# One weight change per subject: where x3T, the two roundings of W0 and their waits stand in the queues

## The chip, the cores and the metric

The kernel runs on one core of one Trainium2 chip. The metric is device time in microseconds (us) of one execution, as the median of several. Times inside an execution are counted from the start of the profiled span.

## The reference, cut to what matters

`x` is 128 samples of 128 tokens with 512 features, float32. Each sample has a subject (8 of them), a category (64), a language and a `delta_t`. Four conditioned layers follow each other, each with a residual:

```python
x = x + (x @ W0[subject].T + b0[subject])
x = x + rotate_pairs(x, a * cos(ang), a * sin(ang))   # pairs of tokens, angle and gain from delta_t
x = x + (x @ W2[category] + b2[category])
h = relu(x @ W1[language] + b1[language])
x = x + layernorm(x + h @ Wup[language] + bup[language]) * gamma[language] + beta[language]
```

## The kernel before, in words

Samples are worked one after another, sorted by subject, so that the weights of the first layer, W0 (512 x 512), are fetched, prepared and kept for all samples of a subject. A table in SBUF, made by the kernel itself, says for each place in the order whether the subject changes there (`is_first`) and how many subjects have begun (`ordinal_of`); engines read it into registers. With 8 subjects there are 7 changes after the start.

Float32 products of layers 0 and 2 are made from two parts in a faster format: ScalarE rounds a tile to its `hi` part, another engine subtracts to get the `lo` part, and TensorE adds x_hi·w_hi, x_lo·w_hi and x_hi·w_lo. Both weight matrices have the identity added first (GpSimd, `fold_w0`, `fold_w2`), which gives the residual. Weights are rounded and subtracted in two halves of 1024 columns.

The five instruction queues are written out by hand, and each works its own in order; they meet at semaphores. Step `s` of the main loop does this:

- **TensorE** (from L825): `l0_front(s + 1)`, the 4 products x_hi·w0_hi (L740) and half of x_lo·w0_hi (L744); `l2(s)`, 12 products (L779, L783, L789, the last 4 waiting for w2_lo by halves); `l0_back(s + 1)`, the other half of x_lo·w0_hi (L751) and x_hi·w0_lo (L757); the transpositions of x3 (L799); `up(s - 1)` (L818); `rotate(s + 1)` (L768), which needs x1 of sample s + 1; `down(s)` (L809), which needs x3T. Then the next step.
- **ScalarE** (from L519): relu (L500), x_hi of sample s + 2 (L458), the diagonal for rotate (L451), w2_hi of s + 1 in two halves (L486), then at a change of subject `round_w0(s + 2)`: under a branch, waits for the folded W0, for layer 0 of s + 1 to be done and for x1 of s + 1; two halves of w0_hi (L462) and a copy of the bias b0 (L463). Then x3T (L507) and x2T_hi of s + 1 (L493).
- **VectorE** (from L687): x2T_lo (L644), w2_lo in two halves (L629), mix (L604), `centre(s - 2)` (L668), x3 of s, called `finish_l2` (L651), yb (L679), x1 of s + 1 (L637), `statistics(s - 1)` (L657, L659, L661: y, bn_stats, bn_aggr), and at a change `rest_of_w0(s + 2)` (L610, w0_lo in two halves).
- **GpSimd** (from L418): rstd (L387, L391), then, once w2_lo of step s is made, x_lo of s + 2 (L381) and the fold of W2 of s + 2 (L375); x3 + bup (L398), + beta (L405), at a change the fold of W0 of s + 3 (L369).
- **SP** issues all loads and stores, up to four samples ahead; the next W0 is fetched into the same buffer once w0_lo and the copy of b0 of the present one are made (`load_w0`, L243).

That x1 of the sample before must be made ahead of the new b0 is because `finish_l0` adds `b0_sb` (L637). That TensorE doesn't use the new w0_hi too early was given by x3T, which ScalarE copied after it, and w0_lo by w2_lo, which VectorE made after it.

## Time and profile before

| | |
|---|---|
| median of 3 runs | 1203.55 us (1201.64 to 1204.3) |
| the profiled execution's own time | 1206.43 us |
| its span | 1204.6 us |
| TensorE matmul busy | 1133.4 us, 94% |
| VectorE busy | 1025.5 us, 85% |
| GpSimd busy | 865.6 us, 72% |
| ScalarE busy | 583.4 us, 48% |
| mean granted TensorE clock | 0.98 |

The span is the time from the first to the last instruction of the execution that the profiler took; the execution's own time is 1.8 us longer. PE is TensorE's matmuls, PEld its weight loads, DVE VectorE, ACT ScalarE, POOL GpSimd, SPq the queue of SyncE. The clock is a share of 2.4 GHz; an average below 1 over a stretch means that it was at 1.2 GHz in part of it. In the profile a buffer's number is left out of its name, so `w_hi` is w0_hi at L462 and w2_hi at L486, and `x` at L651 is x3, at L637 x1.

### The profile page before, as it was taken

The numbers are of one execution on the slowest core, as the hardware profiler recorded it, in microseconds if no ns is written. First come the engines' busy times: TensorE is split into PE (matmuls) and PEld (weight loads), VectorE is DVE, ScalarE is ACT, GpSimd is POOL, SyncE is SP. The second block draws the span as 40 slices with busy tenths as digits, with TensorE's granted clock in tenths as the row PEclk, the third lists the DMA queues.
The fourth block names the chain that finished last, engine by engine and source line by source line (L and its number), as shares of the span: only waits on it lengthen the run. The fifth ranks groups of instructions, "written<-read, shape, count | busy, mean of one in ns | idle before, by whom it ended". The sixth has DMA issues, their size and how long they took to land.

```text
span 1204.6 us, 27886 instructions
## 1 busy us (share of the span) xinstructions
PE 1133.4 (94%) x5902; PEld 913.2 (76%) x5902; DVE 1025.5 (85%) x1465; ACT 583.4 (48%) x923; POOL 865.6 (72%) x792
## 2 busy tenths in 40 slices
PE   1899999999989999999998999989999999999996
PEld 1678878878768887877886788778787887777874
DVE  3398888998888898898888888988888888898887
ACT  2345455455455555445454545445445544544542
POOL 3966667886676677668767666876766677768884
PEclk9899999999999999999999899999998999999999
DMA  6967776777787687767767786787678678867772
GB/s 241 426 225 233 254 258 211 238 253 221 224 291 238 208 261 263 252 213 239 251 215 274 231 259 208 232 286 239 211 249 280 208 237 247 275 214 247 243 252 79
DMA packets 96407, 291.70 MB, mean 242 GB/s; under 512 B 11584, under 2 KB 11712, under 8 KB 78272
## 3 DMA queue, kind: packets, MB, share of 16 engines
q1 hardware_dynamic: 96192, 289.52, 73.3%
q14 instruction: 164, 1.34, 0.3%
q8 instruction: 51, 0.84, 0.3%
HBM read 255.93 MB, written 33.55 MB: 240 GB/s over the span
## 4 chain that ended last, share of the span: by engine, by line
SPq 37%; PE 34%; issue 18%; DVE 5%; DMA 2%; POOL 2%; DVEq 1%; ACT 1%; POOLq 0%; ACTq 0%
SPq L193 6%; SPq L199 5%; SPq L205 5%; PE ps_l L789 4%; PE ps_l L757 4%; PE ps_l L740 4%; PE ps_l L779 4%; PE ps_y L818 3%; PE ps_l L783 3%; PE ps_hT L809 3%; PE ps_mix L768 3%; SPq L196 3%; SPq L208 3%; SPq L202 3%; SPq L286 3%
## 5 line engine op out<-in xcount | busy, mean ns | idle before, releaser
L629 DVE TENSOR_TENSOR w_lo<-w_in,w_hi 128x1024 fp32r<-128x1024 f32 x256 | 330.2, 1330 | 0.0
L381 POOL TENSOR_TENSOR x_lo<-x_in,x_hi 128x512 fp32r<-128x512 f32 x128 | 166.0, 1297 | 160.4 <-DVE w_lo L629 157.1
L486 ACT ACTIVATE w_hi<-w_in 128x1024 fp32r<-128x1024 f32 x256 | 255.3, 1045 | 12.4 <-PE ps_l L783 12.4
L375 POOL TENSOR_TENSOR w_in<-w_in,ident 128x512 f32<-128x512 f32 x128 | 164.3, 1284 | 65.2 <-DMA w_in<-W 64.8
L451 ACT ACTIVATE ps_diag<-ident,cos 128x128 f32<-128x128 f32 x128 | 47.6, 372 | 304.9 <-DVE mix L604 304.6
L405 POOL TENSOR_TENSOR x<-x,beta_sb 128x512 f32<-128x512 f32 x128 | 174.3, 1361 | 28.9 <-POOL x3b L398 28.9
L768 PEld LDWEIGHTS ps_mix<-mix,x 128*128 128x128 f32 x1024 | 132.7, 191 | 73.4 <-issue 69.5
L398 POOL TENSOR_TENSOR x3b<-x,bup_sb 128x512 f32<-128x512 f32 x128 | 169.0, 1320 | 9.6 <-DVE x L651 9.6
L740 PE MATMUL ps_l<-w_hi,x_hi 128*128 128x512 f32 x512 | 154.8, 425 | 15.4 <-ACT w_hi L462 14.1
L789 PE MATMUL ps_l<-w_lo,x2T_hi 128*128 128x512 f32 x512 | 147.7, 401 | 11.6 <-DVE w_lo L629 11.4
L809 PE MATMUL ps_hT<-x3T,w_in 128*128 128x128 f32 x1024 | 138.7, 279 | 13.8 <-ACT x3T L507 13.8
L657 DVE TENSOR_TENSOR ps_y<-ps_y,x3b 128x512 f32<-128x512 f32 x128 | 89.5, 699 | 70.4 <-PE ps_y L818 68.8
L493 ACT ACTIVATE x2T_hi<-ps_mix 128x512 fp32r<-128x512 f32 x128 | 76.3, 596 | 145.5 <-PE ps_mix L768 145.5
L768 PE MATMUL ps_mix<-mix,x 128*128 128x128 f32 x1024 | 136.1, 276 | 7.8 <-DVE x L637 7.6
L779 PE MATMUL ps_l<-w_hi,x2T_hi 128*128 128x512 f32 x512 | 141.0, 398 | 0.0
L809 PEld LDWEIGHTS ps_hT<-x3T,w_in 128*128 128x128 f32 x1024 | 127.0, 195 | 15.7 <-issue 15.7
L757 PE MATMUL ps_l<-w_lo,x_hi 128*128 128x512 f32 x512 | 138.4, 392 | 0.0
L783 PE MATMUL ps_l<-w_hi,x2T_lo 128*128 128x512 f32 x512 | 138.1, 392 | 0.2 <-DVE x2T_lo L644 0.2
L818 PE MATMUL ps_y<-wup_sb,hT 128*128 x256 | 131.1, 594 | 0.8 <-ACT hT L500 0.8
L789 PEld LDWEIGHTS ps_l<-w_lo,x2T_hi 128*128 128x128 f32 x512 | 92.7, 189 | 45.8 <-DVE w_lo L629 29.3
L391 POOL TENSOR_TENSOR rstd<-var_eps,minus_half 128x1 f32<-128x1 f32 x128 | 107.5, 840 | 18.9
L651 DVE TENSOR_TENSOR x<-ps_l,b_in 128x512 f32<-128x512 f32 x128 | 88.5, 692 | 34.3 <-PE ps_l L789 33.8
(82 smaller groups left out, 1713.6 us busy)
## 6 DMA issues: line engine op xcount, KB each, us to landing
w_in<-W SPq DMA_DIRECT2D x128, 1024.0 KB, 6.3
b_in<-b SPq DMA_DIRECT2D x136, 256.0 KB, 5.8
x_in<-xT SPq DMA_DIRECT2D x128, 256.0 KB, 4.8
w_in<-W SPq DMA_DIRECT2D x128, 256.0 KB, 2.7
out<-yb SPq DMA_DIRECT2D x128, 256.0 KB, 5.4
w_in<-W0T SPq DMA_DIRECT2D x8, 1024.0 KB, 4.9
bup_sb<-bup SPq DMA_DIRECT2D x1, 2560.0 KB, 8.8
wup_sb<-Wup SPq DMA_DIRECT2D x1, 2560.0 KB, 10.6
```

The lines of the kernel that those rows point to most:

```text
L398: pool.tensor_tensor(x3b[s % 2][:, :], x3[s % X3B][:, :], bup_sb[:, bass.ds(lang * D, D)], ALU.add)\
L405: pool.tensor_tensor(x3[s % X3B][:, :], x3[s % X3B][:, :], beta_sb[:, bass.ds(lang * D, D)], ALU.add)\
L486: act.activation(w2_hi[:, halves[n]], w2_in[s % WB][:, halves[n]], ACT.Copy).then_inc(w2_hi_made, 1)
L629: dve.tensor_tensor(w2_lo[:, half], w2_in[s % WB][:, half], w2_hi[:, half].bitcast(fp32), ALU.subtract).then_inc(w2_lo_made, 1)
L740: pe.matmul(ps_l0[:, :], x_hi[s % 2][:, c * N:(c + 1) * N], w0_hi[:, c * D:(c + 1) * D], start=(c == 0), stop=False)
L757: mm = pe.matmul(ps_l0[:, :], x_hi[s % 2][:, c * N:(c + 1) * N], w0_lo[:, c * D:(c + 1) * D], start=False, stop=(c == C - 1))
L768: mm = pe.matmul(ps_mix[:, c * N:(c + 1) * N], x1[:, c * P:(c + 1) * P], mix[:, :], start=True, stop=True)
L779: pe.matmul(ps_l2[:, :], x2T_hi[:, c * N:(c + 1) * N], w2_hi[:, c * D:(c + 1) * D], start=(c == 0), stop=False)
L783: mm = pe.matmul(ps_l2[:, :], x2T_lo[:, c * N:(c + 1) * N], w2_hi[:, c * D:(c + 1) * D], start=False, stop=False)
L789: mm = pe.matmul(ps_l2[:, :], x2T_hi[:, c * N:(c + 1) * N], w2_lo[:, c * D:(c + 1) * D], start=False, stop=(c == C - 1))
L809: mm = pe.matmul(ps_hT[:, :], w1_in[s % 2][:, c * A:(c + 1) * A], x3T[:, c * N:(c + 1) * N], start=(c == 0), stop=(c == C - 1))
L818: pe.matmul(ps_y[s % 2][:, :], hT[:, :], wup_sb[:, bass.ds(lang * D, D)], start=True, stop=True)\
```

## The change

ScalarE copies x3T ahead of `round_w0`, and there waits for x1 only before the copy of b0. VectorE makes w0_lo of sample s + 1's subject in step s, between `centre` and `finish_l2`, instead of at the end of step s − 1. TensorE gets waits of its own on w0_hi, b0 and w0_lo, by halves and against the ordinal of the subject, which it reads into a register once per step, between rotate and down; the waits of samples 0 and 1 (both halves of w0_hi; the diagonal) go. w0_lo has a semaphore for each half.

```diff
@@ -155,7 +155,7 @@
         coef_made = sem("coef_made")
         w0_folded = sem("w0_folded")
         w0_hi_made = [sem(f"w0_hi_made{half}") for half in range(2)]
-        w0_lo_made = sem("w0_lo_made")
+        w0_lo_made = [sem(f"w0_lo_made{half}") for half in range(2)]
         b0_made = sem("b0_made")
         x_hi_made = sem("x_hi_made")
         x_lo_made = sem("x_lo_made")
@@ -228,7 +228,8 @@
             sp.dma_start(b1_sb[:, :], b1T).then_inc(b1_loaded, 16)
             sp.dma_start(bup_sb[:, :], bup.rearrange("l d -> (l d)").partition_broadcast(P)).then_inc(bup_loaded, 16)
 
-            sp.sem_inc(w0_lo_made, 2)
+            sp.sem_inc(w0_lo_made[0], 1)
+            sp.sem_inc(w0_lo_made[1], 1)
             sp.sem_inc(b0_made, 1)
             sp.wait_ge(ids_made, 2)
 
@@ -245,7 +246,7 @@
 
                 first, sub, ordinal = is_first(sp, s), subject_of(sp, s), ordinal_of(sp, s)
                 with sp.If(first):
-                    sp.wait_ge(w0_lo_made, 2 * ordinal)
+                    sp.wait_ge(w0_lo_made[1], ordinal)
                     sp.wait_ge(b0_made, ordinal)
                     fetch_w0(sub)
 
@@ -457,24 +458,24 @@
                 act.wait_ge(x_loaded[s % XB], landed(s, XB))
                 act.activation(x_hi[s % 2][:, :], x_in[s % XB][:, :], ACT.Copy).then_inc(x_hi_made, 1)
 
-            def convert_w0():
+            def convert_w0(s):
                 for n, half in enumerate(halves):
                     act.activation(w0_hi[:, half], w0_in[:, half], ACT.Copy).then_inc(w0_hi_made[n], 1)
+                if s >= 1:
+                    act.wait_ge(x1_made, s)
                 act.activation(b0_sb[:, :], b0_in[:, :], ACT.Copy).then_inc(b0_made, 1)
 
-            def round_w0(s):
+            def round_w0(s, first):
 
                 if s == 0:
                     act.wait_ge(w0_folded, 1)
-                    convert_w0()
+                    convert_w0(s)
                     return
-                first = is_first(act, s)
                 with act.If(first):
                     ordinal = ordinal_of(act, s)
                     act.wait_ge(w0_folded, ordinal)
                     act.wait_ge(l0_done, s)
-                    act.wait_ge(x1_made, s)
-                    convert_w0()
+                    convert_w0(s)
 
             def round_w2(s, n):
 
@@ -507,13 +508,13 @@
                 act.activation(x3T[:, :], ps_x3T[:, :], ACT.Copy).then_inc(x3T_made, 1)
 
             round_x(0)
-            round_w0(0)
+            round_w0(0, None)
             make_diag(0)
             round_w2(0, 0)
             round_w2(0, 1)
             round_x(1)
             round_x2T(0)
-            round_w0(1)
+            round_w0(1, is_first(act, 1))
             make_diag(1)
             act.wait_ge(b1_loaded, 16)
 
@@ -528,9 +529,10 @@
                 if s < LAST:
                     round_w2(s + 1, 0)
                     round_w2(s + 1, 1)
+                first = is_first(act, s + 2) if s < LAST - 1 else None
+                copy_x3T(s)
                 if s < LAST - 1:
-                    round_w0(s + 2)
-                copy_x3T(s)
+                    round_w0(s + 2, first)
                 if s < LAST:
                     round_x2T(s + 1)
             relu_hT(LAST, language_of(act, LAST))
@@ -608,7 +610,7 @@
                 for n, half in enumerate(halves):
                     dve.wait_ge(w0_hi_made[n], ordinal)
                     dve.tensor_tensor(w0_lo[:, half], w0_in[:, half], w0_hi[:, half].bitcast(fp32),
-                                      ALU.subtract).then_inc(w0_lo_made, 1)
+                                      ALU.subtract).then_inc(w0_lo_made[n], 1)
 
             def rest_of_w0(s, first):
 
@@ -690,11 +692,13 @@
                 rest_of_w2(s, 1)
                 if s < LAST:
                     make_mix(s + 1)
-                first = is_first(dve, s + 2) if s < LAST - 1 else None
+                first = is_first(dve, s + 1) if 1 <= s < LAST else None
                 if s == 2:
                     dve.wait_ge(gamma_loaded, 16)
                 if s >= 2:
                     centre(s - 2)
+                if 1 <= s < LAST:
+                    rest_of_w0(s + 1, first)
                 finish_l2(s)
                 if s >= 2:
                     finish_norm(s - 2)
@@ -707,8 +711,6 @@
                     dve.wait_ge(coef_made, 4)
                 if s >= 1:
                     statistics(s - 1)
-                if s < LAST - 1:
-                    rest_of_w0(s + 2, first)
             centre(LAST - 1)
             finish_norm(LAST - 1)
             statistics(LAST)
@@ -726,17 +728,14 @@
             pe.matmul(ps_mix[:, 0:B], dt_wide, onehot, start=True, stop=True).then_inc(sorted_done, 1)
             pe.wait_ge(ids_made, 2)
 
-            def l0_front(s):
-
-                if s == 0:
-                    pe.wait_ge(w0_hi_made[0], 1)
-                    pe.wait_ge(w0_hi_made[1], 1)
-                if s == 1:
-                    pe.wait_ge(diag_made, 2)
+            def l0_front(s, ordinal):
+
                 if s >= 1:
                     pe.wait_ge(x1_made, s)
                 pe.wait_ge(x_hi_made, s + 1)
                 for c in range(C):
+                    if c in (0, C // 2):
+                        pe.wait_ge(w0_hi_made[c // (C // 2)], ordinal)
                     pe.matmul(ps_l0[:, :], x_hi[s % 2][:, c * N:(c + 1) * N], w0_hi[:, c * D:(c + 1) * D],
                               start=(c == 0), stop=False)
                 pe.wait_ge(x_lo_made, s + 1)
@@ -744,16 +743,15 @@
                     pe.matmul(ps_l0[:, :], x_lo[s % 2][:, c * N:(c + 1) * N], w0_hi[:, c * D:(c + 1) * D],
                               start=False, stop=False)
 
-            def l0_back(s):
-
+            def l0_back(s, ordinal):
 
                 for c in range(C // 2, C):
                     pe.matmul(ps_l0[:, :], x_lo[s % 2][:, c * N:(c + 1) * N], w0_hi[:, c * D:(c + 1) * D],
                               start=False, stop=False)
-                if s == 0:
-                    pe.wait_ge(b0_made, 2)
-                    pe.wait_ge(w0_lo_made, 4)
+                pe.wait_ge(b0_made, ordinal + 1)
                 for c in range(C):
+                    if c in (0, C // 2):
+                        pe.wait_ge(w0_lo_made[c // (C // 2)], ordinal + 1)
                     mm = pe.matmul(ps_l0[:, :], x_hi[s % 2][:, c * N:(c + 1) * N], w0_lo[:, c * D:(c + 1) * D],
                                    start=False, stop=(c == C - 1))
                 mm.then_inc(l0_done, 1)
@@ -820,17 +818,18 @@
 
             pe.wait_ge(dt_made, 1)
             pe.wait_ge(consts_made, 3)
-            l0_front(0)
-            l0_back(0)
+            l0_front(0, 1)
+            l0_back(0, 1)
             rotate(0)
+            ordinal = ordinal_of(pe, 1)
 
             for s in range(B):
                 lang_before = language_of(pe, s - 1) if s >= 1 else None
                 if s < LAST:
-                    l0_front(s + 1)
+                    l0_front(s + 1, ordinal)
                 l2(s)
                 if s < LAST:
-                    l0_back(s + 1)
+                    l0_back(s + 1, ordinal)
                 transpose_x3(s)
                 if s == 1:
                     pe.wait_ge(wup_loaded, 16)
@@ -838,6 +837,8 @@
                     up(s - 1, lang_before)
                 if s < LAST:
                     rotate(s + 1)
+                if s < LAST - 1:
+                    ordinal = ordinal_of(pe, s + 2)
                 down(s)
             up(LAST, language_of(pe, LAST))
 
```

## Rows read from the trace of the kernel before

**Rows 1.** The page, busy time, share of the span and instructions.

```profile
PE 1133.4 (94%) x5902; PEld 913.2 (76%) x5902; DVE 1025.5 (85%) x1465; ACT 583.4 (48%) x923; POOL 865.6 (72%) x792
```

**Rows 2.** Timeline of an ordinary step (start, length, engine; idle before).

```profile
175.61 1.08 PEld L768 LDWEIGHTS ps_mix<-mix,x 128*128 128x128 f32 x8 [0.45 <-issue]
...
176.98 0.60 ACT L493 ACTIVATE x2T_hi<-ps_mix 128x512 fp32r<-128x512 f32 x1 [1.16 <-PE ps_mix L768]
...
181.99 0.69 DVE L651 TENSOR_TENSOR x<-ps_l,b_in 128x512 f32<-128x512 f32 x1 [0.24 <-PE ps_l L789]
```

**Rows 3.** x3 in ordinary steps, then around the first, fourth, last change: first, last start.

```profile
L651 DVE TENSOR_TENSOR x<-ps_l,b_in x3: 692/692/692, 173.4 to 190.5; 128x512 f32<-128x512 f32 x3
...
L651 DVE TENSOR_TENSOR x<-ps_l,b_in x2: 691/692/692, 161.6 to 173.4; 128x512 f32<-128x512 f32 x2
...
L651 DVE TENSOR_TENSOR x<-ps_l,b_in x2: 692/692/692, 657.5 to 673.2; 128x512 f32<-128x512 f32 x2
...
L651 DVE TENSOR_TENSOR x<-ps_l,b_in x2: 692/692/692, 1048.3 to 1060.3; 128x512 f32<-128x512 f32 x2
```

**Rows 4.** Waits of the whole run: us in total, times, longest.

```profile
DVE x L651 <- PE ps_l L789: 33.8, 79, 7.3
...
PE ps_hT L809 <- ACT x3T L507: 13.8, 7, 2.0
...
ACT w_hi L462 <- DVE x L637: 11.6, 7, 2.8
...
DVE w_lo L610 <- issue: 5.4, 7, 1.3
```

**Rows 5.** Timeline of the third change, and one row of the fourth.

```profile
479.16 2.00 ACT L462 ACTIVATE w_hi<-w_in 128x1024 fp32r<-128x1024 f32 x2 [1.70 <-DVE x L637]
...
481.22 3.69 DVE L610 TENSOR_TENSOR w_lo<-w_in,w_hi 128x1024 fp32r<-128x1024 f32 x2 [0.61 <-issue]
...
481.84 1.99 POOL L405 TENSOR_TENSOR x<-x,beta_sb 128x512 f32<-128x512 f32 x1 [0.23 <-POOL x3b L398]
...
482.07 0.58 ACT L493 ACTIVATE x2T_hi<-ps_mix 128x512 fp32r<-128x512 f32 x1
...
484.83 0.68 DVE L644 TENSOR_TENSOR x2T_lo<-ps_mix,x2T_hi 128x512 fp32r<-128x512 f32 x1
...
485.43 2.34 DVE L629 TENSOR_TENSOR w_lo<-w_in,w_hi 128x1024 fp32r<-128x1024 f32 x2
...
487.70 0.33 DVE L604 SCALAR_TENSOR_TENSOR mix<-signed_swap,sin,ps_diag 128x128 f32<-128x128 f32 x1
...
487.86 1.30 POOL L381 TENSOR_TENSOR x_lo<-x_in,x_hi 128x512 fp32r<-128x512 f32 x1 [2.20 <-DVE w_lo L629]
...
489.11 1.29 POOL L375 TENSOR_TENSOR w_in<-w_in,ident 128x512 f32<-128x512 f32 x1
...
489.27 0.69 DVE L651 TENSOR_TENSOR x<-ps_l,b_in 128x512 f32<-128x512 f32 x1 [0.57 <-PE ps_l L789]
...
661.95 1.13 PE L768 MATMUL ps_mix<-mix,x 128*128 128x128 f32 x8 [1.91 <-DVE x L637]
```

**Rows 6.** SP's issue of a W2 tile at the third change, and its landing (KB, us).

```profile
481.42 0.33 SPq L264 DMA_DIRECT2D w_in<-W  x1
...
w_in<-W SPq DMA_DIRECT2D x1, 1024.0 KB, 6.5
```

**Rows 7.** First and sixth change: us, PE, PEld, DVE, ACT, POOL busy, PEclk, DMA share, GB/s.

```profile
160.00:173.00 13.00, 10.41 (x50) 7.30 (x50) 10.95 (x16) 6.86 (x11) 7.23 (x8) 1.00 0.70 231
921.00:936.00 15.00, 12.20 (x49) 9.65 (x48) 11.15 (x14) 7.39 (x12) 11.54 (x11) 0.77 0.81 276
```

**Rows 8.** Register loads of TensorE (each step) and ScalarE (the ordinal): ns min/median/max.

```profile
L202 PEldq TENSOR_LOAD <-ids x128: 296/302/957, 44.8 to 1194.1; - x128
...
L208 ACTq TENSOR_LOAD <-ids x7: 273/291/1142, 161.7 to 1049.2; - x7
```

**Rows 9.** Timeline near the start, GpSimd.

```profile
33.20 15.63 POOL L416 TENSOR_TENSOR x<-stats_cols,x 128x96 f32<-128x96 f32 x1
```


## The prediction

> **What bounds the kernel now.** I read the page first: TensorE is busy 94% of the span [rows 1]. The timeline of an ordinary step shows that this isn't the whole bound [rows 2]. The step repeats every 8.55 us (x3 at 173.4, 182.0 and 190.5, [rows 2, 3]). TensorE's weights for rotate are loaded as soon as x1 is there, at 175.61, and it has no hole from there to the next x3. VectorE waits for TensorE for only 0.24 us before the next x3. Two chains of nearly equal length close in every step, so delay put on either one counts.
>
> The seven changes of subject cost extra. There the distance from one x3 to the next is 11.8 us in the first (161.6 to 173.4), 15.7 in the fourth and 12.0 in the seventh and last [rows 3]; the seven together are 94.6 us, 34.8 over seven steps of 8.54. Outside this sum, 2.9% of the time, there is little for the change to win.
>
> The waits name what happens [rows 4]: ScalarE waits 11.6 us for x1 before it rounds W0, `down` then waits 13.8 us for x3T behind it, both seven times. The timeline of the third change gives the order [rows 5]: w0_hi 479.16, x2T_hi 482.07 (0.58 long), w0_lo 481.22 to 484.91, x2T_lo 484.83, w2_lo 485.43, mix 487.70, x3 489.27. So w0_lo holds VectorE back while x2T_hi is already there, and the wait of `down` is not itself the end of the chain.
>
> **The change, part by part.** *ScalarE.* The same four operations (x3T, two halves of w0_hi, b0) still stand ahead of x2T_hi; they take 2.91 us from the first start to x2T_hi [rows 5]. What goes is the wait for x1. What comes is the taken branch and its load of the ordinal, formerly hidden behind that wait: VectorE shows 0.6 to 1.3 us for the same pair (5.4 over seven, [rows 4]), of which x3T's 0.5 us covers most; I take 0.3, between 0 and 0.8. Release to start costs another 0.1. So 11.6 − 7 × 0.4 = 8.8 us. It loses 0.7 where the transposition ends up to 0.3 us after w2_hi, and 0.7 where rotate, which starts with x1, ends too late: in the fourth change rotate runs 661.95 to 663.08 [rows 5], so x2T_hi can start at 663.2 and not at 662.5, where ScalarE's own work would have it. **x2T_hi comes earlier by 7.4 us in total.** b0 keeps the wait for x1, which has ended by then.
>
> *VectorE.* w0_lo leaves the place ahead of x2T_lo and stands, one step of TensorE's order later, between centre and the next x3. Old, from x2T_hi's start to that x3: 7.20 us in the third change (482.07 to 489.27) and 51.5 over all seven. New: 0.69 to x2T_lo (x2T_hi's 0.60 and a release), 2.87 to mix (484.83 to 487.70), then w0_lo in series. Here GpSimd matters, since it starts x_lo 0.16 us after mix, for 1.30, and then folds the next W2 for 1.29 [rows 5]. That the two engines don't run such operations side by side is seen where w0_lo meets the beta addition: 3.69 us for the pair of halves and 1.99 for the addition, while a pair alone takes 2.34 (w2_lo). So the first half starts when x_lo ends (mix + 1.46) and ends at mix + 2.6; the second ends at + 3.8 if the fold has not landed by then, and at + 5.0 if it has and takes its turn. In the third change x2T_hi comes 1.2 us earlier, at 480.9, mix at 484.4, and mix + 2.6 is 487.0; the tile to be folded is issued at 481.42 and lands 6.5 us later, at 487.9: no collision [rows 6]. Worked out likewise three of the seven collide, and two more miss by under 0.3 us. Seven times 0.69 + 2.87 + 3.85, plus 3 × 1.25, is 55.6. **This chain gets 4.1 us longer**; with no collision at all it would be 3.1 shorter (3.35 in place of 3.85), with all seven 9.1 longer.
>
> *Clock.* Over the sixth change the granted clock is 0.77 on average, which is partly 1.2 GHz and partly 2.4, over the first 1.00 [rows 7]. The first has one long idle time of TensorE, before `down`; the others have two close together, as 1.91 us before rotate in the fourth [rows 5] and 2.0 before `down` [rows 4]. The loss is small in the old order (x3 waits for TensorE 0.57 us in the third change, 0.24 in an ordinary step), because VectorE is late there in any case. The new order takes away the idle before `down`, but TensorE now stops ahead of the w0_lo products: done with its x_lo part at mix + 0.95, it gets the first half at + 2.6, the second at + 3.8 or + 5.0, and x3 for its transpositions after that. That is 2.7 to 4 us idle in 3.6 to 4.9. I expect about five falls, now just before work that has no slack: the gapless step. A stretch like the old ones, of 3 to 4 us at 1.2 GHz, halves what is done in it and costs 1.3 to 1.7. **+7.0 us**, between 0 and 15. The Trainium skill ("TensorE: Matmul & The Clock Gate", Part 1: The HAM clock gate) gives the half rate as the state after a whole idle stretch of its monitor. By that rule pieces of idleness broken by matmuls would leave the clock up, and the sum would be about 1200.8 us; rows 7 with rows 5 speak against it, since the clock fell with rotate between two idle times.
>
> *Every step.* The untaken branch leaves the place between bn_aggr and x2T_lo, some 0.1 us where VectorE binds (it does in 49 of 128 steps, since TensorE releases x3 in 79, [rows 4]); most of those exceed 8.54 by less: −1.0, between 0 and −5. TensorE gets one more register load per step, between rotate and down, and register waits. A load takes 0.30 us, at most 0.96 [rows 8], and with its arithmetic and check about 0.65; rotate's passes occupy 1.0 us after 0.25 us of issue. It just fits, and the load for the language behind it as well; only the odd long ones show. +1.5 us, between 0 and 12 (0.1 in each of 120 steps). ScalarE's load and branch lie before its idle 1.16 us for rotate [rows 2]: nothing. SP's wait uses a count reached many samples before: nothing.
>
> *Start.* `l0_front(0)` no longer waits for both halves, and `l0_front(1)` not for diag; that is at most some 4 us by x3 of sample 0. Both are swallowed: x_lo of sample 2, without which `l0_front(2)` can't go on, stands behind GpSimd's power of 15.63 us, which ends at 48.8 whatever TensorE does [rows 9]. 0, between −1.5 and +1.5.
>
> **Sum:** −7.4 + 4.1 + 7.0 − 1.0 + 1.5 = +4.2 us on the profiled execution's 1206.43 (span 1204.6), 2.9 above the median shown; on the median 1203.55 that is 1207.8. A measurement of this kernel can tell about 0.2%, 2.4 us, from no change.
>
> **The rivals.**
> *The clock stays up* (0.20). Everything as above without the 7 us: 1200.8, range 1198 to 1203. For it: the 2 us before `down` in the first change left the clock at full [rows 7]. Against it: the new idle pieces are longer and closer.
> *The ports don't collide and the clock stays* (0.10). w0_lo takes 2.35 us directly behind centre: 48.4 for the chain, 3.1 less than before, and 7.4 + 3.1 + 1.0 − 1.5 = 10.0 us gained: 1193.6. Against it is the 3.69 beside 2.34 [rows 5].
> *The effects cancel* (0.20). Falls of the clock, fewer or half covered by the idle time, cost 2 to 5 us: 1202 to 1206. The change then only moves the same stall from `down` to the w0_lo products.
> *TensorE's queue* (0.10), the far side. The load between rotate and down, with the wait behind it, delays the first weights of down. rotate is issued only as x1 arrives, so the queue starts each step empty. It decides from a delay of 0.05 us per step, and 0.1 gives +12: 1219 with the rest. In this place the gapless step [rows 2] has no cover.
> *Code behind the taken branch*, part of the forecast's upper range: ScalarE's load of the ordinal took up to 1.14 us, with a median of 0.29 [rows 8]. If each taken branch of ScalarE showed 1.3 us, x2T_hi would lose 7 us: 1214.8. The Trainium skill ("Runtime: NRT & Kernel Launch", Instruction fetch mechanics) says that a taken branch out of the fetched pages stalls until its page is loaded; no row here shows that as a rule: VectorE's seven waits add up to only 5.4 us.
>
> **How the numbers follow.** Forecast as worked out: 0.40, its own range 1204 to 1215. Faster is the two first rivals, 0.30; same is the cancelling one and the forecast's low edge, 0.22; slower the rest, 0.48. The range leaves out the far ends of the second and fourth rival: 1196 to 1216.
>
> **What would show it.** `down` no longer waits for x3T; x2T_hi stands 0.1 to 1.7 us nearer to the x3 before it; w0_lo follows centre and its pair takes 2.8 us or more; TensorE's longest waits at a change are for w0_lo of W0; the granted clock is below 1 after the new x3 and no more before it; ordinary steps stay at 8.54. The forecast is wrong if x3 to x3 falls under 12.5 us in all seven changes, if the clock stays at 1.00 there, or if ordinary steps grow.

## The result, and the profile after

The changed kernel takes 1215.13 us (median of 9 runs, 1206.18 to 1217.9), the kernel before beside it 1202.43 (9 runs). The ratio is 1.0091, with a 95% interval of 1.0071 to 1.0111: **slower by 10.9 us**, where 4.2 were forecast. The profiled execution took 1216.06 us, 9.6 more than that of before.

The head of its page:

```profile
span 1214.2 us, 28514 instructions
...
PE 1137.1 (94%) x5902; PEld 916.4 (75%) x5902; DVE 1011.1 (83%) x1465; ACT 585.8 (48%) x923; POOL 842.1 (69%) x792
```

The busy times are those of before [rows 1] within 0.5% on TensorE and ScalarE; VectorE's is 1.4% lower and GpSimd's 2.7%. Less busy time makes no kernel slower, so look at waits and at order. TensorE's waits:

```profile
PE ps_l L755 <- DVE w_lo L612: 20.5, 15, 2.0
PE ps_l L739 <- ACT w_hi L463: 13.2, 1, 13.2
...
PE ps_mix L766 <- DVE x L639: 8.8, 7, 1.9
```

The 13.8 us of `down` behind x3T [rows 4] are gone, and 20.5 us in 15 pieces have come, in which the w0_lo products wait for VectorE (the 13.2 is the start). The timeline of the third change, the answer to [rows 5] (start us, us, engine and line):

```profile
479.25 0.69 DVE L653 TENSOR_TENSOR x<-ps_l,b_in 128x512 f32<-128x512 f32 x1 [0.43 <-PE ps_l L787]
...
481.73 2.00 ACT L463 ACTIVATE w_hi<-w_in 128x1024 fp32r<-128x1024 f32 x2
...
484.38 0.60 ACT L494 ACTIVATE x2T_hi<-ps_mix 128x512 fp32r<-128x512 f32 x1
...
485.45 1.29 POOL L406 TENSOR_TENSOR x<-x,beta_sb 128x512 f32<-128x512 f32 x1 [0.23 <-POOL x3b L399]
...
485.68 3.28 DVE L631 TENSOR_TENSOR w_lo<-w_in,w_hi 128x1024 fp32r<-128x1024 f32 x2
...
488.89 0.33 DVE L606 SCALAR_TENSOR_TENSOR mix<-signed_swap,sin,ps_diag 128x128 f32<-128x128 f32 x1
...
489.81 4.11 DVE L612 TENSOR_TENSOR w_lo<-w_in,w_hi 128x1024 fp32r<-128x1024 f32 x2
490.58 2.25 POOL L376 TENSOR_TENSOR w_in<-w_in,ident 128x512 f32<-128x512 f32 x1
...
491.85 0.70 PE L755 MATMUL ps_l<-w_lo,x_hi 128*128 128x512 f32 x2 [1.64 <-DVE w_lo L612]
...
493.85 0.68 DVE L653 TENSOR_TENSOR x<-ps_l,b_in 128x512 f32<-128x512 f32 x1
...
493.98 1.06 PE L755 MATMUL ps_l<-w_lo,x_hi 128*128 128x512 f32 x2 [1.42 <-DVE w_lo L612]
...
495.68 1.92 PE L816 MATMUL ps_y<-wup_sb,hT 128*128 x2
```

The order is the one the change wants. But VectorE and GpSimd now meet twice: w2_lo meets the beta addition (3.28 us for a pair of halves that takes 2.34 alone, [rows 5]), and w0_lo meets x_lo and the fold (4.11). And behind the new x3 the up-projection takes 1.92 us where it took 1.02 one step earlier: TensorE runs at 1.2 GHz. That is so around every new x3 of a change. The windows (length, busy times of TensorE, its weight loads, VectorE, ScalarE and GpSimd, then the granted clock):

```profile
173.00:181.00 8.00, 6.03 (x25) 4.23 (x26) 6.05 (x8) 1.63 (x3) 4.29 (x5) 0.79 0.59 208
354.00:362.00 8.00, 5.87 (x24) 4.07 (x25) 6.21 (x8) 1.33 (x3) 4.16 (x3) 0.79 0.64 209
491.00:499.00 8.00, 5.72 (x24) 3.94 (x25) 6.10 (x7) 1.50 (x3) 4.37 (x3) 0.79 0.76 249
...
672.00:680.00 8.00, 6.11 (x26) 4.01 (x25) 6.12 (x7) 2.15 (x4) 4.56 (x3) 0.79 0.74 239
808.00:820.00 12.00, 8.94 (x35) 6.50 (x34) 9.19 (x11) 3.90 (x7) 6.64 (x6) 0.72 0.66 221
938.00:946.00 8.00, 5.55 (x22) 3.78 (x23) 6.10 (x7) 1.50 (x3) 4.56 (x3) 0.79 0.79 252
1064.00:1076.00 12.00, 8.60 (x33) 6.23 (x33) 9.19 (x11) 3.46 (x6) 6.70 (x6) 0.72 0.56 185
```

Reading every x3 off the timeline, the two traces differ like this:

| | before | after | difference |
|---|---|---|---|
| from the start to x3 of sample 1 | 56.9 | 55.4 | −1.5 |
| the seven changes, x3 to x3 | 94.6 | 101.9 | +7.3 |
| of these: x3 to x2T_hi | 43.1 | 36.7 | −6.4 |
| of these: x2T_hi to the next x3 | 51.5 | 65.3 | +13.8 |
| the seven steps right behind them | 59.9 | 71.4 | +11.5 |
| all other steps, above 8.545 us each | 23.4 | 15.6 | −7.8 |

Before rounding that makes +9.6, the whole difference of the two executions. The last line called for an explanation; a second trace of the kernel before (h_before_again, below) has 14.6 there. It differs at the changes too: 99.4 us from x3 to x3, of which 45.3 up to x2T_hi and 54.2 behind it, while the seven steps right behind them are 59.9 again. So single traces of one kernel differ by some 9 us in the other steps and by 5 at the changes. Against this second trace the part up to x2T_hi is 8.6 us shorter in the changed kernel and the part behind it 11.1 longer; only the 11.5 of the steps right behind is the same by both. The smaller effects had to be timed.

### The profile page after: what moved, and what is told of

It is laid out like the page before. It is cut to its first block, busy times and chain, and to the rows that moved or that the text cites. A ratio compares the mean times of both kernels' runs of the same rounds, so it can differ in the third digit from the quotient of the medians.

```text
span 1214.2 us, 28514 instructions
## 1 busy us (share of the span) xinstructions
PE 1137.1 (94%) x5902; PEld 916.4 (75%) x5902; DVE 1011.1 (83%) x1465; ACT 585.8 (48%) x923; POOL 842.1 (69%) x792
## 3 DMA queue, kind: packets, MB, share of 16 engines
q14 instruction: 164, 1.34, 0.3%
## 4 chain that ended last, share of the span: by engine, by line
PE 55%; SPq 21%; issue 13%; DVE 5%; DMA 3%; DVEq 1%; POOL 1%; ACT 1%; ACTq 0%; POOLq 0%
PE ps_l L755 6%; PE ps_l L739 6%; PE ps_mix L766 6%; PE ps_y L816 6%; PE ps_l L787 6%; PE ps_l L777 6%; PE ps_l L781 5%; PE ps_hT L807 5%; SPq L193 3%; PE ps_x3T L797 3%; SPq L199 3%; PE ps_l L743 3%; PE ps_l L749 3%; SPq L205 3%; DMA b_in<-b 2%
## 5 line engine op out<-in xcount | busy, mean ns | idle before, releaser
L631 DVE TENSOR_TENSOR w_lo<-w_in,w_hi 128x1024 fp32r<-128x1024 f32 x256 | 317.4, 1280 | 0.0
L487 ACT ACTIVATE w_hi<-w_in 128x1024 fp32r<-128x1024 f32 x256 | 255.6, 1046 | 12.2 <-PE ps_l L781 11.1
L376 POOL TENSOR_TENSOR w_in<-w_in,ident 128x512 f32<-128x512 f32 x128 | 171.2, 1337 | 39.5 <-DMA w_in<-W 39.4
L766 PEld LDWEIGHTS ps_mix<-mix,x 128*128 128x128 f32 x1024 | 137.5, 196 | 76.2 <-issue 72.3
L406 POOL TENSOR_TENSOR x<-x,beta_sb 128x512 f32<-128x512 f32 x128 | 167.4, 1308 | 28.9 <-POOL x3b L399 28.2
L399 POOL TENSOR_TENSOR x3b<-x,bup_sb 128x512 f32<-128x512 f32 x128 | 163.5, 1277 | 21.4 <-DVE x L653 21.0
L739 PE MATMUL ps_l<-w_hi,x_hi 128*128 128x512 f32 x512 | 150.7, 416 | 15.6 <-ACT w_hi L463 13.2
L755 PE MATMUL ps_l<-w_lo,x_hi 128*128 128x512 f32 x512 | 142.4, 398 | 20.5 <-DVE w_lo L612 20.5
L787 PE MATMUL ps_l<-w_lo,x2T_hi 128*128 128x512 f32 x512 | 141.4, 393 | 5.7 <-DVE w_lo L631 5.7
L816 PE MATMUL ps_y<-wup_sb,hT 128*128 x256 | 137.2, 619 | 0.8 <-ACT hT L501 0.8
L755 PEld LDWEIGHTS ps_l<-w_lo,x_hi 128*128 128x128 f32 x512 | 95.7, 190 | 45.9 <-DVE w_lo L612 13.6
L508 ACT ACTIVATE x3T<-ps_x3T 128x512 f32<-128x512 f32 x128 | 76.4, 597 | 96.4 <-PE ps_x3T L797 95.5
## 6 DMA issues: line engine op xcount, KB each, us to landing
wup_sb<-Wup SPq DMA_DIRECT2D x1, 2560.0 KB, 11.1
```

Source lines behind the costliest of these rows:

```text
L376: pool.tensor_tensor(diagonal_of(w2_in[s % WB]), diagonal_of(w2_in[s % WB]), ident[:, :].unsqueeze(1).broadcast_to([P, C, P]), ALU.add).th ...
L406: pool.tensor_tensor(x3[s % X3B][:, :], x3[s % X3B][:, :], beta_sb[:, bass.ds(lang * D, D)], ALU.add)\
L487: act.activation(w2_hi[:, halves[n]], w2_in[s % WB][:, halves[n]], ACT.Copy).then_inc(w2_hi_made, 1)
L631: dve.tensor_tensor(w2_lo[:, half], w2_in[s % WB][:, half], w2_hi[:, half].bitcast(fp32), ALU.subtract).then_inc(w2_lo_made, 1)
L739: pe.matmul(ps_l0[:, :], x_hi[s % 2][:, c * N:(c + 1) * N], w0_hi[:, c * D:(c + 1) * D], start=(c == 0), stop=False)
L755: mm = pe.matmul(ps_l0[:, :], x_hi[s % 2][:, c * N:(c + 1) * N], w0_lo[:, c * D:(c + 1) * D], start=False, stop=(c == C - 1))
```

## The experiments

Each was timed beside the kernel before, and is given as the ratio of the two medians with its 95% interval; 0.1% is 1.2 us. The edits are to the changed kernel unless said otherwise, and cut to the lines that matter (`...`).

**First four: one part at a time, and the clock.** a_waits_only has ScalarE's and VectorE's old order, with SyncE's wait, TensorE's waits and the start of the change. b_act_only adds ScalarE's new order to it, c_dve_only VectorE's. d_filled is the changed kernel with filler for TensorE.

```diff
# a: ScalarE and VectorE as before
-                first = is_first(act, s + 2) if s < LAST - 1 else None
+                if s < LAST - 1:
+                    round_w0(s + 2, is_first(act, s + 2))
                 copy_x3T(s)
-                if s < LAST - 1:
-                    round_w0(s + 2, first)
...
-                if 1 <= s < LAST:
-                    rest_of_w0(s + 1, first)
...
+                if s < LAST - 1:
+                    rest_of_w0(s + 2, first)
# d: ahead of each half of the w0_lo products, n = 6 and 7, result unused
+                with pe.If(first):
+                    pe.wait_ge(x3T_made, s - 1)
+                    for k in range(n):
+                        pe.matmul(ps_x3T[:, :], x_hi[s % 2][:, 0:N], w0_hi[:, 0:D], start=True, stop=True)
```

> TensorE's new waits and its register load alone; ScalarE and VectorE keep the order of before. Theory 1 (the loss is w0_lo in series with x3, its meetings with GpSimd, and the clock that falls behind it): within 2 us of the kernel before, the seven changes as before (94.6 us from x3 to x3), the step behind a change 8.55 us. Theory 2 (the load and the waits on TensorE's queue cost a little in every step): 3 us or more slower, and ordinary steps above 8.55.

> As the changed kernel, but VectorE makes w0_lo where it did before, at the end of the step. Theory 1: x3 to x2T_hi keeps the gain of 6.5 us over seven changes; w0_lo still begins behind the statistics and is 3.4 to 3.7 us long beside the beta addition, so most of the gain is lost in front of x2T_lo: 1 to 4 us faster than before, and no step behind a change above 8.6. Theory 2: slower than before by what the waits alone cost.

> As the changed kernel, but ScalarE keeps the order and the wait of before. Theory 1: slower than the changed kernel by 2 to 8 us, since the gain of ScalarE's order (6.5 us) is gone while w0_lo stays in series; w2_lo starts about 1 us later and meets the beta addition less, which gives back up to 5; the steps behind the changes are 9.8 to 11 us long as in the changed kernel. Rival: ScalarE's new order is what costs, then this is near the kernel before.

> The changed kernel, in which TensorE, at a change of subject, runs 6 products of its own ahead of the first half of w0_lo and 7 ahead of the second, into a buffer that is free then (they add nothing to the result). If the clock is what makes the seven steps behind a change 1.2 to 2.5 us longer, they return to about 8.55 to 8.8 us, the granted clock stays at 1.00 from one change to the next, and the whole is 7 to 11 us faster than the changed kernel. If something else delays those steps, they stay at 9.8 to 11 us.

Measured: a 0.9924 (0.9902 to 0.9947), b 0.9953 (0.9934 to 0.9971), c 1.002 (1.0001 to 1.004), d 0.9963 (0.9948 to 0.9977). a was expected level and is 9 us faster than before: what I had costed near nothing isn't nothing. ScalarE's order alone costs 3.5 us (b less a, the intervals overlap), VectorE's place 11.5 (c less a). b was expected 1 to 4 us faster than before and is 5.6 faster. c was expected 2 to 8 us slower than the changed kernel and is 8.5 faster, so beside VectorE's new place ScalarE's new order costs 8.5. The trace of c shows one reason. Its x2T_hi comes 4.2 us later over the seven changes than in the changed kernel (40.9 behind x3 in place of 36.7), and so w2_lo misses the beta addition in six of the seven; from x2T_hi to mix it takes 25.2 us in place of 30.5. Its w2_lo in the third change:

```profile
482.66 2.35 DVE L629 TENSOR_TENSOR w_lo<-w_in,w_hi 128x1024 fp32r<-128x1024 f32 x2
```

The steps right behind the changes are shorter in c as well, 65.7 us in place of 71.4. d takes 15.4 us off the changed kernel (1.0091 to 0.9963). Its windows over the first and the third change, and VectorE and TensorE in the third:

```profile
160.00:176.00 16.00, 15.60 (x76) 11.84 (x75) 13.72 (x18) 9.70 (x15) 12.13 (x11) 1.00 0.85 286
470.00:490.00 20.00, 19.16 (x95) 14.36 (x93) 16.75 (x22) 10.47 (x16) 13.28 (x12) 1.00 0.81 279
```

```profile
485.64 3.85 DVE L612 TENSOR_TENSOR w_lo<-w_in,w_hi 128x1024 fp32r<-128x1024 f32 x2
...
487.89 1.75 PE L751 MATMUL ps_x3T<-w_hi,x_hi 128*128 128x512 f32 x7
...
489.41 0.68 DVE L653 TENSOR_TENSOR x<-ps_l,b_in 128x512 f32<-128x512 f32 x1
...
497.75 0.69 DVE L653 TENSOR_TENSOR x<-ps_l,b_in 128x512 f32<-128x512 f32 x1 [0.46 <-PE ps_l L797]
```

The pair of w0_lo still takes 3.85 us, yet the clock stays at 1.00 and the next step takes 8.34 us (489.41 to 497.75); in the changed kernel it is 9.83 (493.85 to 503.68). The seven next steps together are 58.7 in place of 71.4. So the slow steps come from the clock, and the clock falls no more once TensorE's idle pieces ahead of the w0_lo products are filled. That was expected at 7 to 11 us and gave 15.4; the 12.7 of the seven next steps are the part that the trace ties to the clock.

**Next four: where a's gain comes from.** g_sp_only and e_start_only are edits to the kernel before, f_waits_old_start is a with the old start, h is the kernel before unchanged.

```diff
# g: one semaphore for each half; SyncE waits on the second (every other line as before)
-                    sp.wait_ge(w0_lo_made, 2 * ordinal)
+                    sp.wait_ge(w0_lo_made[1], ordinal)
# e: l0_front(0), l0_front(1), l0_back(0) wait by halves
+                    if s <= 1 and c in (0, C // 2):
+                        pe.wait_ge(w0_hi_made[c // (C // 2)], ordinal)
# f: in a
+                if s == 0:
+                    pe.wait_ge(w0_hi_made[0], 1)
+                    pe.wait_ge(w0_hi_made[1], 1)
+                if s == 1:
+                    pe.wait_ge(diag_made, 2)
```

> The kernel before with the new waits of the first two samples alone (the first products wait for W0 by halves, sample 1 waits for its W0 and not for the diagonal). Theory A (the 9 us that the waits alone brought come from the start, which puts TensorE 3.7 us ahead of the loads and leaves the rest of the pipeline in another phase): all of it here, 7 to 11 us faster, and the excess of ordinary steps over 8.55 us falls from about 23 us to about 13. Theory B (they come from the register waits in every step): no difference over 2 us. Theory C (they come from SP's semaphore): no difference either.

> The waits-only kernel with the start of before (both halves of W0 for sample 0, the diagonal for sample 1, and one register load per step as there). Theory A: as the kernel before, or up to 2 us slower by the loads. Theory B: 7 to 11 us faster than before. Theory C: the same, as SP's semaphore is there too.

> The kernel before with w0_lo's semaphore split into two, so that SP waits for the ordinal and not for twice the ordinal; nothing else. Theory C: 7 to 11 us faster. Theories A and B: within 2 us of before.

> The kernel before, unchanged: what a second trace of it differs from the first by. If the ordinary steps' excess (23 us over 8.55 us in the first trace) is its own, it is 20 to 26 again; if it is chance of one execution, it may be anywhere from 10 to 25, and then differences of that size between single traces say nothing, and the timed medians alone decide. Ratio to before within 0.2% of 1.

Measured: e 0.9988 (0.9972 to 1.0004), f 0.9936 (0.9915 to 0.9957), g **0.9884** (0.9866 to 0.9902), h 0.999 (0.9974 to 1.0006). The one line of SyncE is worth 13.9 us, more than the 7 to 11 expected. The waits and the load that TensorE got in every step cost 6.2 of it again (f less g); the start gives 1.4, not told apart from nothing.

**Then: which part of these lines.** j_sp_doubled is g with the doubling put back and every wait at the same moment. i_load_moved is a with TensorE's load elsewhere. k_fold_waits removes the meeting of w0_lo and fold. l_sp_and_start has SyncE's line and the start alone.

```diff
# j: in g
-                    sp.wait_ge(w0_lo_made[1], ordinal)
+                    sp.wait_ge(w0_lo_made[1], 2 * ordinal)
...
-                                      ALU.subtract).then_inc(w0_lo_made[n], 1)
+                                      ALU.subtract).then_inc(w0_lo_made[n], 1 + n)
# i: in a
                     l0_back(s + 1, ordinal)
+                if s < LAST - 1:
+                    ordinal = ordinal_of(pe, s + 2)
                 transpose_x3(s)
...
-                if s < LAST - 1:
-                    ordinal = ordinal_of(pe, s + 2)
                 down(s)
# k: GpSimd
+                    ordinal = ordinal_of(pool, s + 1)
                     rest_of_x(s + 2)
+                    pool.wait_ge(w0_lo_made[1], ordinal + 1)
                     fold_w2(s + 2)
```

> g_sp_only with one thing put back: VectorE counts its second half by two, and SyncE waits for twice the ordinal again, so that the moment of every wait is that of g_sp_only and the doubling instruction is back 19 times in SyncE's code, in a branch that runs seven times. Theory (the size of SyncE's code makes a second stop of 1.4 us behind each turn of its loop): the second stop is back and the ratio is that of the kernel before, 0.997 to 1.001. Rival (two semaphores in place of one, or the moment of the wait, made the difference): the ratio stays at 0.987 to 0.990 and there is no second stop. Second rival (the saving is in fewer executed instructions): 7 instructions fewer in all could give at most some tenths of a microsecond, so 0.988 as well.

> The kernel of a_waits_only with TensorE's register load of the next ordinal moved from between rotate and down, where it stands directly ahead of the language load of the next step, to behind l0_back, ahead of the transposes. In the trace of f_waits_old_start the two loads stand one behind the other while the last weights of down go in (0.30 and 0.65 to 0.86 us), and the first weights of l0_front follow 0.4 us late in steps of 8.6 to 9.1 us; with one load there the queue keeps its lead. Theory (the two loads in a row cost the 6 us between f_waits_old_start and g_sp_only): the steps fall back to 8.55 us and the ratio goes from 0.9924 to 0.986 to 0.989. Rival (the waits themselves cost it, wherever the load stands): 0.991 to 0.995. Second rival (the load costs as much in its new place, in front of the transposes, which start as soon as x3 is there): 0.993 to 0.999.

> The changed kernel with GpSimd's fold of the next W2 held until VectorE has made w0_lo (a register load and a wait a step on GpSimd, satisfied at once outside the changes). Theory (in the changed kernel w0_lo and the fold slow each other at all seven changes): w0_lo's two halves take 2.4 to 2.5 us in place of 3.8 to 4.4, x3 comes some 1.5 us earlier at each change, and the ratio goes from 1.009 to 0.998 to 1.003; TensorE's clock may fall as often as before. Rival (the fold, held up, delays the rounding of the next W2 and the beta addition by as much, so that the next step pays): 1.005 to 1.012. Slower still if GpSimd's register load of 0.3 to 0.9 us a step makes rstd late: over 1.012.

> The order of before on every engine, with the two parts of the change that gained: SyncE's wait on the second half's own semaphore, and the start that waits by weight halves. No register load or new wait on TensorE in the 125 steps behind the start. If the two gains add (13.9 us and 1.4 us): 1184 us on a kernel before of 1199.5, ratio 0.986 to 0.989. If the gain of g_sp_only hangs on how SyncE's code happens to lie, which this kernel shares with it, the same. Rival (the start's gain is not real): 0.988 to 0.990, level with g_sp_only.

Measured: j 0.999 (0.9976 to 1.0004), i 0.9898 (0.9876 to 0.9921), k 1.0042 (1.0026 to 1.0057), l 0.9895 (0.9875 to 0.9914).

j is level with the kernel before, and with h: by j less g the doubling is worth 12.7 of the 13.9 us, and the rest is within the intervals. j isn't quite SyncE's line alone, since counting by two gives VectorE one more semaphore instruction at each w0_lo (3545 of its instructions in the trace against 3537 in g); o_changed_padded, below, changes SyncE alone. The doubling stands 19 times in SyncE's code, in a branch that is taken seven times: 3 places in the start, 4 in the steps ahead of the loop, 12 in the loop's body. SyncE's issues behind a turn of its loop, in g and then in j:

```profile
188.98 0.34 SPq L281 DMA_DIRECT2D w_in<-W  x1
193.57 0.34 SPq L265 DMA_DIRECT2D w_in<-W  x1
```

```profile
188.77 0.34 SPq L281 DMA_DIRECT2D w_in<-W  x1
194.89 0.34 SPq L265 DMA_DIRECT2D w_in<-W  x1
```

The next W2 is issued 4.59 us after W1 in g and 6.12 in j. SyncE's own instructions show why. Here is the first jump back of its loop in g: the jump, the first instruction behind it, and the check of the register load that follows. The same in j comes next, with the instruction just ahead of the check as well (lengths in ns, then first and last start in us):

```profile
L325 SPq COMPARE_BRANCH  x1: 53/53/53, 189.4 to 189.4; - x1
L325 SPq FUSED_REGOPS  x1: 64/64/64, 192.6 to 192.6; - x1
L199 SPq SEQ_ASSERT  x1: 24/24/24, 193.2 to 193.2; - x1
```

```profile
L325 SPq COMPARE_BRANCH  x1: 45/45/45, 189.3 to 189.3; - x1
L325 SPq FUSED_REGOPS  x1: 64/64/64, 192.4 to 192.4; - x1
L199 SPq FUSED_REGOPS  x1: 166/166/166, 192.9 to 192.9; - x1
L199 SPq SEQ_ASSERT  x1: 24/24/24, 194.5 to 194.5; - x1
```

Behind the jump it stands still for 2.8 to 3.2 us in both, and in j (as in before) once more for 1.4 to 1.7, at each of the nine jumps back. It hardly catches up: behind the first jump in g its next six W2 issues follow one another by 8.4 to 8.8 us, against a step of 8.55. So it is late for steps; GpSimd's fold is the first to feel it. Its row on the page (busy, mean | idle before it) in before's second trace h, in j, in g, in a and in the changed kernel:

```profile
L375 POOL TENSOR_TENSOR w_in<-w_in,ident 128x512 f32<-128x512 f32 x128 | 164.4, 1284 | 56.0 <-DMA w_in<-W 55.5
```

```profile
L376 POOL TENSOR_TENSOR w_in<-w_in,ident 128x512 f32<-128x512 f32 x128 | 164.5, 1285 | 54.2 <-DMA w_in<-W 53.5
```

```profile
L376 POOL TENSOR_TENSOR w_in<-w_in,ident 128x512 f32<-128x512 f32 x128 | 165.2, 1290 | 27.8 <-DMA w_in<-W 27.3
```

```profile
L376 POOL TENSOR_TENSOR w_in<-w_in,ident 128x512 f32<-128x512 f32 x128 | 165.6, 1294 | 16.5 <-DMA w_in<-W 16.5
```

```profile
L376 POOL TENSOR_TENSOR w_in<-w_in,ident 128x512 f32<-128x512 f32 x128 | 171.2, 1337 | 39.5 <-DMA w_in<-W 39.4
```

For i and f, read the idle time before TensorE's weight loads of l0_front, over the whole run (behind the second bar: in all, then what ended most of it). In g, in f, in a (with `down`'s weight loads above) and in i:

```profile
L741 PEld LDWEIGHTS ps_l<-w_hi,x_hi 128*128 128x128 f32 x512 | 89.1, 195 | 27.2 <-issue 14.5 <-ACT ps_diag L452 1.6
```

```profile
L742 PEld LDWEIGHTS ps_l<-w_hi,x_hi 128*128 128x128 f32 x512 | 89.8, 196 | 33.6 <-issue 20.1 <-ACT ps_diag L452 1.6
```

```profile
L805 PEld LDWEIGHTS ps_hT<-x3T,w_in 128*128 128x128 f32 x1024 | 126.2, 194 | 15.9 <-issue 15.7
...
L737 PEld LDWEIGHTS ps_l<-w_hi,x_hi 128*128 128x128 f32 x512 | 88.8, 194 | 30.1 <-issue 17.9 <-ACT w_hi L463 0.4
```

```profile
L737 PEld LDWEIGHTS ps_l<-w_hi,x_hi 128*128 128x128 f32 x512 | 89.2, 195 | 24.7 <-issue 13.3 <-ACT w_hi L463 0.4
```

f has 6.4 us more than g there, and is 6.2 slower. i, with the load moved, has 5.4 less than a, of which 3.1 show in the time, with intervals that overlap. The place is not `down`, where I had looked (15.9 in a, 15.7 in i): two register loads in a row run while the queue works through down's weights, and l0_front's come too late. The second of them, for the language, has a median of 0.30 us in all these traces, but in one step of ten it takes 0.91 or more in f and a, and in i no more than about 0.36.

k took 5.9 us off the changed kernel, and w0_lo went from 1989 ns a half to 1664 (seven changes and the start):

```profile
L612 DVE TENSOR_TENSOR w_lo<-w_in,w_hi 128x1024 fp32r<-128x1024 f32 x16 | 31.2, 1989 | 0.0
```

```profile
L614 DVE TENSOR_TENSOR w_lo<-w_in,w_hi 128x1024 fp32r<-128x1024 f32 x16 | 26.0, 1664 | 0.0
```

It stayed above the 2.5 us that I expected for the pair, because the first half still meets x_lo. The clock fell as often: at all seven changes. l is level with g: the start adds nothing to it.

**Last three: do the causes add?** m_filled_fold_waits has the edits of d and k, n_and_load_moved that of i as well. o_changed_padded is the changed kernel with the doubling put back in SyncE's branch:

```diff
+                    sp.wait_ge(x_hi_made, 2 * ordinal)
                     sp.wait_ge(w0_lo_made[1], ordinal)
```

> The changed kernel with both remedies at once: the filler products of d_filled, and GpSimd's fold held until w0_lo is made, of k_fold_waits. Apart they moved the ratio from 1.0091 to 0.9963 (15 us) and to 1.0042 (6 us). Theory (the moves on ScalarE and VectorE cost 20 us by a slower clock and by the meeting of w0_lo with the fold, two separate causes): the two add, 0.989 to 0.993, level with a_waits_only (0.9924), where nothing is moved. Rival (both remedies act on one and the same delay, since a shorter change is also a shorter rest for TensorE): no more than the better of the two, 0.995 to 0.998.

> m_filled_fold_waits with TensorE's load of the ordinal moved behind l0_back as well. i_load_moved gained 3 us by this on a_waits_only (0.9924 to 0.9898). Theory (a third separate cause): 2 to 4 us less than m_filled_fold_waits. Rival (in the changed kernel the load stands behind the filler's branch and its register load and costs nothing or more there): no gain, or a loss.

> The changed kernel with the doubling instruction put back in SyncE's branch: a further wait there, for twice the ordinal on ScalarE's count of rounded samples, which is far higher by then, so that it never holds anything up; all other engines as changed. Theory (the changed kernel has gained what g_sp_only shows, and its two moves have lost 20 us against that): the second stop of 1.4 us behind each of the nine turns of SyncE's loop is back, and the ratio goes from 1.009 to 1.016 to 1.022. Rival (the changed kernel doesn't depend on SyncE, because its changes of subject wait for other things; then the gain of 14 us never reached it and the moves cost about 10 us): the stops are back and the ratio stays at 1.007 to 1.012.

Measured: m 0.9948 (0.993 to 0.9965), n 0.991 (0.9888 to 0.9932), o 1.0139 (1.0115 to 1.0163). m is only 1.8 us better than d, with intervals that overlap. That looks like one delay seen twice, the meeting making the idle pieces long enough to cost the clock, but m doesn't show it. Its clock is at 1.00 and x2T_hi to x3 is 3.4 us shorter than in d (57.7 against 61.1); the seven steps behind take 65.1 in place of 58.7 and lose it again. The third change, w0_lo, the second piece of filler and the products behind it:

```profile
486.00 3.31 DVE L614 TENSOR_TENSOR w_lo<-w_in,w_hi 128x1024 fp32r<-128x1024 f32 x2
488.80 1.76 PE L753 MATMUL ps_x3T<-w_hi,x_hi 128*128 128x512 f32 x7
490.40 0.62 PE L767 MATMUL ps_l<-w_lo,x_hi 128*128 128x512 f32 x2
```

w0_lo is done at 489.31 and its products start at 490.40: seven filler products are right for d and 1 us too long here. How far the two causes add with shorter filler is untested. TensorE's load is worth 4.6 us in m (n less m, expected 2 to 4; the intervals just touch). o is between its theories: the nine second stops are back, and they cost 5.8 us here and not 13.9. So the changed kernel had SyncE's gain, but less than half of it. A likely reason is that at its changes it waits for VectorE while SyncE catches up: SyncE waits for x3 51.1 us in 48 places there, and 20.3 in 27 in g.

## Why the prediction was wrong in size

**The sign was right, and the number was too small.** +4.2 us was the sum, +10.9 is the result. It lies inside the range given by luck: a gain on SyncE that the sum did not have hides part of the loss, and with the doubling put back (o) the change costs 16.8 us, outside the range. By its steps:

- *x2T_hi earlier by 7.4 us.* 6.4 by the first trace of before, 8.6 by the second. Right, with its reason.
- *"This chain gets 4.1 us longer."* **This step failed**: it got 13.8 longer (11.1 by the second trace of before). Two errors. The part from x2T_hi to mix was taken as 0.69 + 2.87, 24.9 us for all seven, and is 30.5: w2_lo, moved forward, now meets the beta addition, which the old order had let w0_lo meet. I moved w0_lo off the beta addition and never asked what took its place; c, where w2_lo misses it in six of seven, has 25.2. And "three of the seven collide" with the fold: all seven do, and mix to x3 is 34.8 us in place of 30.7. This doesn't hang on the first error, since all seven collide in c too; the tile was there earlier than I had worked out (in the third change issued 4.7 us behind x3, and 5.5 before). k shows this meeting by itself: 5.9 us of time, and 29.6 from mix to x3, which is also more than the 27.0 (7 × 3.85) that I had taken without the fold.
- *Clock +7.0.* The mechanism is shown by d, the size was low: 7 falls and not 5, two of them long, 11.5 us in the trace and 15.4 by d. The falls of before were also read too short in part: the 0.77 over 15 us of [rows 7] is some 7 us at 1.2 GHz (15 × 2 × 0.23), not 3 to 4. In the third change TensorE's idle pieces are 1.34 us before rotate (2.14 for its weight loads), and 1.64 and 1.42 before the w0_lo products. The rule of the Trainium skill ("TensorE: Matmul & The Clock Gate", Part 1: The HAM clock gate), half rate after a whole idle stretch of its monitor, would have given 1200.8; here the clock fell with matmuls between every two pieces of idleness, so the trace does not agree with it as I had read it.
- *TensorE's register load +1.5.* Measured 3.1 (i less a), 4.6 (n less m) and, with the waits, 6.2 us (f less g); only the last is clear of the intervals. It is a part of the rival "TensorE's queue". The decision point was well placed (6.2 us are 0.05 a step), the victim was l0_front and not `down`.
- *"SP's wait uses a count reached many samples before: nothing."* **The second step that failed**, in the other direction: −13.9 us alone, −5.8 in the changed kernel. I asked when the wait ends and not what its line compiles to, nor whether SyncE has slack.
- *Start 0.* −1.5 in the trace, −1.4 (e) and +1.3 (l less g) by the clock of the runs: right.
- *Branch −1.0.* Not told apart; the spread of other steps between two traces of before (23.4 and 14.6) is larger.

Put together from the runs, as an estimate that takes n less m for the changed kernel: SyncE −5.8, TensorE's load about +4.6, start about −1; so the two moves cost about 13, where the forecast had 3.7 − 1.0. The +20 between a and the changed kernel contains some 8 us (13.9 less 5.8) of SyncE's gain that is lost with them. In both pairs that tell, VectorE's new place loses: 11.5 us (c less a) and 16.6 (the changed kernel less b). ScalarE's new order costs 3.5 (b less a, not clear) and 8.5 beside VectorE's new place (the changed kernel less c), although it brings x2T_hi forward as forecast.

**The best version** is g_sp_only, one line on SyncE with the semaphore that it needs: 1185.34 us, 14 faster than the kernel before and about 25 faster than the changed one. l (0.9895) and i (0.9898) are not told apart from it.

## What to carry to other kernels

An operation that is moved off one collision is a collision for whatever follows it: go through the neighbours again with the new times, on the engine itself and on the one that slows it when both run (here VectorE and GpSimd). Ask of the queue that issues transfers how much slack it has in a step, and count a line of register arithmetic in its loop as a change of its code, however seldom it runs. Where TensorE must idle in pieces, a few unused matmuls in the holes can be cheaper than the clock, as in d; size them anew when the hole changes, as m shows.

## What the runs showed that I had not expected

- **One register instruction in a branch that is seldom taken moved a kernel by 12.7 us** (j less g; g against the kernel before is 13.9). The jump back of SyncE's loop costs 2.7 to 3.2 us each time (3.4 once), and with the 19 more instructions of the doubling a second stop of 1.4 to 1.7 us follows, nine times of nine. So it does wherever the doubling stands, in before, e, h, j and o, and in none of the others. The Trainium skill ("Runtime: NRT & Kernel Launch", Instruction fetch mechanics) says that code is fetched in blocks ahead of use, and that a jump out of the blocks at hand stalls until its block is there. The first stop agrees with it. The second sits at a place of the code, and not at an operation: in before, e and h it stands ahead of the fifth instruction behind the jump; in j and o, whose programs have one instruction more ahead of the loop, ahead of the fourth; in g, with seven fewer than j there, ahead of the eleventh, and is 0.37 to 0.56 us long. That this place is where the next block begins, reached too soon behind the jump, fits all of these and is not shown directly.
- **Unused matmuls gave 15.4 us** (d): 91 of them, 13 at each of seven changes, kept the clock at 1.00 and made the changed kernel 4 us faster than the one before.
- **A queue's lead can be worth 0.05 us a step**: two register loads behind one another in TensorE's queue showed not at the weights right behind the first of them but at the next group (6.4 us of idle time in f over g, 6.2 in the time).
